# A feed-forward part whose second product is issued inside the next batch's first phase

## The reference, cut to what matters

```python
def act_quant(x):      # per token, to int8 steps
    scale = 127.0 / jnp.clip(jnp.max(jnp.abs(x), axis=-1, keepdims=True), 1e-05)
    return jnp.clip(jnp.round(x * scale), -128, 127) / scale
def weight_quant(w):   # to -1, 0, 1
    scale = 1.0 / jnp.clip(jnp.mean(jnp.abs(w)), 1e-05)
    return jnp.clip(jnp.round(w * scale), -1, 1) / scale
def _L0_ffn_ref(x, w1, conv_w, conv_b, w2):      # x is already layer-normed
    h = bit_linear(x, w1)                        # (4, 1024, 512) -> (4, 1024, 2048)
    h = depthwise_conv1d(h.transpose(0, 2, 1), conv_w, conv_b)   # 3 taps over tokens
    h = jax.nn.silu(h.transpose(0, 2, 1))
    return bit_linear(h, w2)                     # -> (4, 1024, 512)
x = x + jnp.tanh(g_ffn[0]) * _L0_ffn_ref(_layernorm(x), ...)
```

## Time and profile before

| | us |
|---|---|
| median of the three runs | 1868.02 |
| the profiled execution, its time | 1868.89 |
| its span in the profile | 1867.1 |
| TensorE busy | 1669.6 (89%) |
| VectorE busy | 1204.4 (65%) |
| ScalarE busy | 827.8 (44%) |
| GpSimd busy | 719.0 (39%) |
| mean granted TensorE clock | 0.965 of full |

### The profile page before, as it was taken

One profiled execution on the slowest core, in us unless ns is written; L12 is line 12 of the kernel. 1 busy time (PEld: TensorE's weight loads), 2 busy tenths in 40 slices (PEclk: granted clock), 3 DMA queues, 4 the chain that ended last, 5 costly groups with the idle time before them and its releaser, 6 DMA issues. The chain is left out here.

```text
span 1867.1 us, 23800 instructions
## 1 busy us (share of the span) xinstructions
PE 1669.6 (89%) x8754; PEld 1026.6 (55%) x8754; DVE 1204.4 (65%) x2205; ACT 827.8 (44%) x866; POOL 719.0 (39%) x314
## 2 busy tenths in 40 slices
PE   6888899999999999999999999999986876877758
PEld 5666678888886544454445444544453433444434
DVE  6777645443345667657865786667359478399793
ACT  2111222222220344424562456345647767677666
POOL 1131000000000488856875687567825043151340
PEclk9999999999999999999999999999999897998989
DMA  6656456544434411202231213221331020200201
GB/s 238 238 186 213 168 193 223 176 160 152 157 130 158 148 58 67 98 20 103 98 106 48 102 59 113 69 103 36 128 136 53 23 90 23 89 2 1 91 0 46
DMA packets 107811, 200.81 MB, mean 108 GB/s; under 512 B 7616, under 2 KB 33216, under 8 KB 107712
## 3 DMA queue, kind: packets, MB, share of 16 engines
q1 hardware_dynamic: 107712, 199.49, 30.4%
HBM read 124.75 MB, written 74.71 MB: 107 GB/s over the span
## 5 line engine op out<-in xcount | busy, mean ns | idle before, releaser
L726 POOL TENSOR_TENSOR acc<-acc,pr 128x1024 f32<-128x1024 f32 x188 | 448.3, 2385 | 134.4 <-ACT pr L756 117.8
L756 ACT ACTIVATE pr<-ps,mcol 128x1024 f32<-128x1024 f32 x256 | 284.4, 1115 | 366.5 <-PE ps L1452 363.9
L1014 DVE CUSTOM_DVE_ANT_0 junk<-ps,mbias 128x512 bf16<-128x512 f32 x512 | 333.1, 688 | 129.3 <-PE ps L1427 125.2
L1464 PE MATMUL ps<-pr,vv 128*64 128x512 f32 x1024 | 274.7, 618 | 0.0
L731 POOL TENSOR_TENSOR h_first<-h_first,last_tap 128x1024 f32<-128x1024 f32 x44 | 104.8, 2386 | 274.0 <-ACT last_tap L897 274.0
L707 POOL MEMSET nmt<- 128x128 f32 x1 | 0.2, 204 | 364.2 <-DVE chl L1227 364.2
L1427 PE MATMUL ps<-kh,qh 64*128 64x512 f32 x512 | 123.0, 452 | 13.1 <-DVE nmv L1014 12.0
L1533 PE MATMUL ps<-xiT,w1q 128*128 128x512 bf16 x512 | 123.8, 389 | 5.0 <-ACT xiT L746 5.0
L726 POOL TENSOR_TENSOR acc<-pr 128x1024 f32<-128x1024 f32 x32 | 76.8, 2401 | 122.0 <-ACT pr L756 122.0
L1427 PEld LDWEIGHTS ps<-kh,qh 64*128 64x128 f32 x512 | 51.0, 185 | 130.9 <-issue 99.3
L1690 PE MATMUL ps<-w2q,hq 128*128 128x512 bf16 x512 | 121.2, 390 | 1.5 <-ACT hq L925 0.8
(11 more groups left out here) (173 smaller groups left out, 3218.8 us busy)
## 6 DMA issues: line engine op xcount, KB each, us to landing
craw<-in_ctxT SPq DMA_DIRECT2D x8, 2048.0 KB, 9.6
xa<-in_x SPq DMA_DIRECT2D x8, 1024.0 KB, 6.2
wraw<-in_w1T SPq DMA_DIRECT2D x16, 512.0 KB, 7.6
wraw<-in_w2T SPq DMA_DIRECT2D x16, 512.0 KB, 8.1
q_split<-kqh SPq DMA_DIRECT2D x32, 256.0 KB, 2.0
q_split<-kql SPq DMA_DIRECT2D x32, 256.0 KB, 2.3
base<-lna SPq DMA_DIRECT2D x8, 1024.0 KB, 9.1
k_split<-kqh SPq DMA_DIRECT2D x32, 256.0 KB, 2.1
```

The costliest lines, as they stand in the source:

```text
L726: nc.gpsimd.tensor_tensor(acc[:, blk % 2, :], first, pr[:, (8 * blk + j) % NP, :], ALU.add).then_inc(pool_acc, 1)
L756: act.activation(pr[:, u % NP, :], ps[:, 2 * (u % 2):2 * (u % 2) + 2, :].rearrange("p a t -> p (a t)"), ACT.Exp, bias=mcol[:, (u // 64) * ...
L1014: dve.tensor_tensor_reduce(out=(junk1 if n < LEAD and n % 2 else junk)[:, e, :], in0=ps[:, first_bank(n) + e, :], in1=mbias[:, b % 2, kk * ...
L1464: last = pe.matmul(ps[64 * e:64 * e + 64, 6 + blk % 2, :], vv[g % 2][:, j, 64 * e:64 * e + 64], pr[:, u % NP, e * CH:(e + 1) * CH], start= ...
```

## The change

A batch's second product is no longer a phase of its own. In the first phase of the next batch, block j issues half of a token tile of the previous batch's second product: the half q = j, eight transposes (`turn_h(b - 1, j)`), a copy (`turned`) and eight matmuls (`second(b - 1, j - 1)`, one block later). Only the last batch's second product stands alone, in half tiles too. The rounded hidden values are kept for a whole batch, as int8 in `h8`, which VectorE writes straight from `hT` in eight instructions between two first phases; GpSimd converts them to bfloat16 (`to_bf16`), a token tile at a time, in two buffers `hb`.

The convolution works on PSUM: `dve_scaled` writes back into the pair of banks, the taps read from there (`pair(j)`), shifted by slices and without padding, and `gp` is gone. VectorE's tap now comes before GpSimd's add, and `pe_first` of block j + 2 waits for VectorE's tap of block j. The turns of `h` use banks 4 and 5 only; bank 6 takes in turn the halves of `turn_h`, the halves of the next batch's row and the turns of its input; bank 7 takes the second product.

`row` and `xiT` become two buffers each. The next batch's row and turns stand in blocks 8 to 13 of the first phase. The eight layer-norm steps of batch 3 stand in the first phase of batch 0, after blocks 1, 2 and 4 to 9 (`STEP_AT`), and its integers go through DRAM as those of the other batches do. `x2` is loaded and the output stored a token tile at a time. In the diff only added and kept lines are shown, since the removed ones stand above.

```diff
+        row = [sb("row0", [P, S], F32), sb("row1", [P, S], F32)]
+        xiT = [sb("xiT0", [P, KD, S], BF16), sb("xiT1", [P, KD, S], BF16)]
+        h = [sb("h_first", [P, S], F32), sb("h_second", [P, S], F32)]
+        assert used["at"] <= CHL + SLOT
         used["at"] = CHL + SLOT
         x2 = sb("x2t", [P, NT, D], F32)
         used["at"] = XN
+        h.append(sb("h_third", [P, S], F32))
+        last_tap = [sb("last_tap0", [P, S], F32), sb("last_tap1", [P, S], F32)]
+        LAST_NORM = used["at"]
+        h8 = sb("h8", [P, NT, HID], INT8)
...
+        STEP_AT = (1, 2, 4, 5, 6, 7, 8, 9)
+        STD_AT = 4
...
+        def pair(j):
+            return ps[:, 2 * (j % 2):2 * (j % 2) + 2, :].rearrange("p a t -> p (a t)")
...
+            def load_x2(b, i):
+                r = (b * NT + i) * P
+                sp.dma_start(x2[:, i, :], x2_d[r:r + P, :]).then_inc(sp_x2_in[i], 16)
+
+            for i in range(NT):
+                load_x2(0, i)
             load_xn(B - 1)
+            for b in range(B + 1):
+                if b + 1 < B:
+                    sp.wait_ge(pe_xt, (b + 1) * (NT // 2))
                     load_xi(b + 1)
+                if b == 0:
+                    sp.wait_ge(dve_ln, LN_DVE_N)
+                    sp.dma_start(xi_d[(B - 1) * S:B * S, :].rearrange("(j p) d -> p j d", p=P), xi3[:]).then_inc(sp_xi_out, 16)
+                    continue
+                for i in range(NT):
+                    r = ((b - 1) * NT + i) * P
+                    sp.wait_ge(dve_d, D_DVE[f"o{b - 1}_{i}"])
+                    sp.dma_start(out[r:r + P, :], x2[:, i, :]).then_inc(sp_out, 16)
+                    if b < B:
+                        sp.wait_ge(sp_out, 16 * ((b - 1) * NT + i + 1))
+                        load_x2(b, i)
+            sp.wait_ge(sp_out, 16 * B * NT)
...
+            def to_bf16(b, i):
+                pool.wait_ge(dve_d, D_DVE[f"q{b}_{i}"])
+                if i >= 2:
+                    pool.wait_ge(pe_ht, b * KH + 2 * i - 2)
+                elif b:
+                    pool.wait_ge(pe_ht, b * KH - 2 + 2 * i)
+                nc.gpsimd.tensor_copy(hb[:, i % 2, :], h8[:, i, :]).then_inc(pool_bf, 1)
+
+            for b in range(B):
                 for j in range(KH):
+                    pool.wait_ge(act_d, D_ACT[f"u{b}_{j}"])
+                    pool.wait_ge(dve_d, D_DVE[f"c{b}_{j}"])
+                    nc.gpsimd.tensor_tensor(h[(b * KH + j) % 3][:, 0:S - 1], h[(b * KH + j) % 3][:, 0:S - 1], last_tap[j % 2][:, 0:S - 1], ALU.add).then_inc(pool_tap, 1)
+                    if b and j % 2 == 0 and 2 <= j < KH - 2:
+                        to_bf16(b - 1, j // 2 + 1)
+                to_bf16(b, 0)
+                to_bf16(b, 1)
+            for i in range(2, NT):
+                to_bf16(B - 1, i)
...
+            def taps(b, j):
+                act.wait_ge(dve_d, D_DVE[f"g{b}_{j}"])
+                if b * KH + j >= 3:
+                    act.wait_ge(pe_ct, b * KH + j - 2)
+                act.activation(h[(b * KH + j) % 3][:], pair(j), ACT.Identity, bias=convb[:, j:j + 1],
+                               scale=convw[:, j, 1:2]).then_inc(act_d, 1)
+                if b * KH + j >= 2:
+                    act.wait_ge(pool_tap, b * KH + j - 1)
+                act.activation(last_tap[j % 2][:, 0:S - 1], pair(j)[:, 1:S], ACT.Copy, scale=convw[:, j, 2:3]).then_inc(act_d, 1)
+
+            def turned(b, q):
+                i, t = q // 2, q % 2
+                act.wait_ge(pe_ht, b * KH + q + 1)
+                if b * NT + i >= 2:
+                    act.wait_ge(pe_o, b * NT + i - 1)
+                act.activation(hq[:, i % 2, 8 * t:8 * t + 8].rearrange("p j t -> p (j t)"), ps[:, 6, :].bitcast(BF16),
+                               ACT.Copy).then_inc(act_d, 1)
+
+            taps(0, 0)
+            taps(0, 1)
+            for b in range(B):
                 for j in range(KH):
                     if j + 2 < KH:
+                        taps(b, j + 2)
                     act.wait_ge(pe_ct, b * KH + j + 1)
+                    if b and j == 0:
+                        act.wait_ge(dve_d, D_DVE[f"q{b - 1}_{NT - 1}"])
+                    act.activation(hT[:, :, j * P:(j + 1) * P], ps[:, 4:6, :].rearrange("p a (i t) -> p (a i) t", t=P),
                                    ACT.Silu).then_inc(act_d, 1)
+                    if b:
+                        turned(b - 1, j)
+                    if b == 0 and j == STD_AT:
+                        act_ln_std(act, B - 1)
+                    if b + 1 < B and j in (8, 9):
+                        act_ln_row(act, b + 1, j - 8)
+                    if b + 1 < B and 10 <= j < 10 + NT // 2:
+                        act_ln_turned(act, b + 1, j - 10)
+                if b + 1 < B:
+                    taps(b + 1, 0)
+                    taps(b + 1, 1)
+            for q in range(KH):
+                turned(B - 1, q)
...
+            steps = ln_steps(dve, B - 1)
+            for b in range(B):
                 for j in range(KH):
+                    done(f"g{b}_{j}")
+                    dve.wait_ge(act_d, D_ACT[f"u{b}_{j}"])
+                    dve.scalar_tensor_tensor(out=h[(b * KH + j) % 3][:, 1:S], in0=pair(j)[:, 0:S - 1], scalar=convw[:, j, 0:1], in1=h[(b * KH + j) % 3][:, 1:S],
+                                             op0=ALU.mult, op1=ALU.add).then_inc(dve_d, 1)
+                    if j >= 2:
+                        biggest(b, j - 2)
+                    if b and j >= 3 and j % 2:
+                        finish2(b - 1, (j - 3) // 2)
                     if j + 2 < KH:
                         dve_scaled(dve, b, j + 2)
+                    if b == 0 and j in STEP_AT:
+                        steps[STEP_AT.index(j)]()
+                    if b + 1 < B and j == 6:
+                        dve.wait_ge(pe_row, 2 * b + 1)
+                        dve_diagonal(dve, b + 1)
+                if b + 1 < B:
+                    dve_scaled(dve, b + 1, 0)
+                biggest(b, KH - 2)
+                biggest(b, KH - 1)
+                if b:
+                    finish2(b - 1, NT - 1)
+                    done(f"o{b - 1}_{NT - 1}")
+                done(f"hmax{b}_{KH - 1}")
                 dve.tensor_reduce(hm[:], hmax[:].rearrange("p j i -> p i j"), AX.X, ALU.max).then_inc(dve_d, 1)
+                done(f"hm{b}")
                 dve.tensor_scalar(hm[:], hm[:], 1e-5, None, ALU.max).then_inc(dve_d, 1)
+                done(f"hmc{b}")
                 dve.reciprocal(hsc[:], hm[:]).then_inc(dve_d, 1)
+                done(f"hrec{b}")
                 dve.tensor_scalar(hsc[:], hsc[:], 127.0, None, ALU.mult).then_inc(dve_d, 1)
                 dve.tensor_scalar(hdq[:], hm[:], deq2, None, ALU.mult).then_inc(dve_d, 1)
+                done(f"hdq{b}")
+                if b:
+                    dve.wait_ge(pool_bf, b * NT)
+                else:
+                    dve.wait_ge(sp_xi_out, 16 * B)
                 for i in range(NT):
+                    dve.tensor_scalar(h8[:, i, :], hT[:, i, :], hsc[:, i:i + 1], None, ALU.mult).then_inc(dve_d, 1)
+                    if i == 1 and b + 1 < B:
+                        dve_scaled(dve, b + 1, 1)
+            for i in range(NT):
+                finish2(B - 1, i)
...
+            if b == 0:
+                for t in range(2):
+                    last = pe.matmul(ps[:, 2 + t, :], ones[:], diag[:, 4 * t:4 * t + 4, :], start=True, stop=True)
+                last.then_inc(pe_row, 1)
+            else:
+                pe.matmul(ps[:, 6, :], ones[:], diag[:, 4 * half:4 * half + 4, :], start=True, stop=True).then_inc(pe_row, 1)
...
+                pe.wait_ge(dve_d, D_DVE[f"c{b}_{j - 2}"])
+            elif b:
+                pe.wait_ge(dve_d, D_DVE[f"c{b - 1}_{KH - 2 + j}"])
+            if b and j == 0:
+                pe.wait_ge(act_ln, LN_ACT[f"xT{b}_{NT // 2 - 1}"])
             for t in range(2):
                 for k in range(KD):
+                    last = pe.matmul(ps[:, 2 * (j % 2) + t, :], w1q[:, k, j * P:(j + 1) * P], xiT[b % 2][:, k, t * 512:(t + 1) * 512],
...
+            def turn_h(b, q):
+                i, t = q // 2, q % 2
+                if t == 0:
+                    pe.wait_ge(pool_bf, b * NT + i + 1)
+                for j in range(8 * t, 8 * t + 8):
+                    last = pe.transpose(ps[:, 6, :].bitcast(BF16)[:, (j % 8) * P:(j % 8 + 1) * P], hb[:, i % 2, j * P:(j + 1) * P], identb[:])
+                last.then_inc(pe_ht, 1)
+
+            def second(b, q):
+                i, t = q // 2, q % 2
+                pe.wait_ge(act_d, D_ACT[f"hq{b}_{q}"])
+                if t == 0 and b * NT + i:
+                    pe.wait_ge(dve_d, D_DVE[f"o{b}_{i - 1}" if i else f"o{b - 1}_{NT - 1}"])
+                for j in range(8 * t, 8 * t + 8):
+                    last = pe.matmul(ps[:, 7, :], hq[:, i % 2, j, :], w2q[:, j, :], start=j == 0, stop=j == KH - 1)
+                if t:
+                    last.then_inc(pe_o, 1)
+
+            def turn_free(b, j, last_use):
```

(80 more changed lines are left out.)

285 lines of the change are left out of this document (65 added, 220 removed).

## The result

| | kernel before | kernel after |
|---|---|---|
| median, us | 1867.98 (1863.62 to 1870.0, 4 runs) | 1929.57 (1926.86 to 1933.58, 4 runs) |
| profiled execution, us | 1868.89 | 1933.58 |
| span of the profile, us | 1867.1 | 1931.8 |

The changed kernel takes 1.0335 times as long (95% interval 1.0306 to 1.0363), 62 us more. The forecast was 1916.5 in a range of 1878 to 1945: the sign and the mechanism came out, the size is 13 us short of the median.

A forecast was written before the change was run, and what follows sets the result against it. Bound: a chain of waits through all engines, 5.20 us a block. Batch 0 to 1508.5, two batches of 117.7, batch 3's 88.6, tail 63.1: 1895.6; casts 9, clock 11: span 1915.6, forecast 1916.5, range 1878 to 1945.

The forecast's parts named there:

- one chain of waits through all engines: Blocks of batches 1 to 3: waits running through the engines and back take 10.40 us per two blocks, 5.20 each.
- the clock term: TensorE falling to 1.2 GHz after waits: 11 us in all, 1.5 of it after xn; between nothing and 25.
- Blocks without a norm step: Batch 0's first phase: VectorE's taps and TensorE's first product wait on each other, 4.38 us a block against 4.05.
- the stall: Batch 0, before the first layer-norm statistics: VectorE stands waiting for the DMA of xn, 14.1 us.
- The blocks with row halves: Blocks in batches 1 and 2 issuing half of the next batch's row, waiting for ScalarE's copy: 8.15 us each.
- those with a turn: Blocks in batches 1 and 2 turning the next batch's input, waiting for ScalarE's copy: 7.77 us each.
- Roundings and casts: Batch ends: eight roundings and VectorE's next tap 12.0 us; GpSimd's casts beside them 3 more, three times, 9 in all.
- the rival of roundings at one column a cycle: Batch ends: int8 roundings of 2048 columns take 2.35 us, giving 1942; chance 0.10.
- Tail: Last batch's second product standing alone: 3.46 us a half block with one turn bank, against 2.17; sum 63.1.
- PE is never late behind ScalarE: Rival: blocks at TensorE's own 4.84 us, tail at 2.17 a half block, giving 1854, faster; chance 0.10.
- Slow casts: Rival: GpSimd's casts as slow as its two-input add, 4.8 us each, giving 1937; chance 0.06.
- xn in time: Rival for batch 0: xn lands in time or its wait costs half, 1902 to 1909; no separate chance given.

The follow-up runs named there:

- the two edits together: Kernel after, last batch's second product only: turn of h issued before the product, and output accumulators alternating between banks 7 and 0; 1911.52 us, ratio 1.0236.
- the kernel with all remedies: Kernel after with turns before products, row halves and turns right behind F, layer-norm steps later, casts behind the last rounding, two output banks in the tail; 1848.97 us.

## Why the prediction was right, and where it fell short

The forecast of 1915.6 for the span stands against 1931.8. The mechanism held: one chain of waits through all engines sets each block. The step that was mis-sized is a term of the sum, the clock in batch 0. By stretches:

| term, casts and clock put in | forecast | measured |
|---|---|---|
| C(0) of batch 0 ends | 1387.9 | 1388.65 |
| batch 0 to its first rounding | 110.1 | 122.4 |
| roundings to C(0), three times | 45.1 | 42.3 |
| batches 1 and 2, to the first rounding | 216.2 | 223.5 |
| batch 3, likewise | 91.1 | 89.35 |
| tail | 65.1 | 65.6 |

**Batch 0, the step that was mis-sized: the clock term.** Its parts came out where they had been put. Blocks without a norm step 4.41 (4.38), and the stall, forecast at 14.1:

```profile
1409.96 2.47 DVE L984 BATCH_NORM_STATS2 st<-xn 128x6 f32<-128x512 f32 x4 [13.68 <-DMA xn<-x]
1412.35 1.27 DVE L1365 SCALAR_TENSOR_TENSOR h_third<-ps,convw,h_third 128x1023 f32<-128x1023 f32 x1
...
1413.68 3.59 PE L1562 MATMUL ps<-xiT,w1q 128*128 128x512 bf16 x8 [16.01 <-DVE h_third L1365]
```

(xn was issued at 1398.26 and is what ends VectorE's idle time; C(2) and F(4) stand behind.) But the last row shows F at 3.59 where 1.89 was put, the lower level of the clock, 1.2 GHz. The forecast gave 1.5 us to this clock after the stall and named the gaps of the norm steps only for the upper end. The granted clock was 0.68 and 0.74 over 78 us: F waits for C, C for a norm step, TensorE stands about half of each block, and F, on the chain, takes 1.1 to 1.7 more in seven of the blocks. From C(0) to C(14) that made 109.1 against 98.4. In the run with matmuls without use this part took 99.9, near the forecast without the clock term: the gain came with the raised clock, while VectorE's steps stayed as they were. The other 3 us of batch 0 lie at its end, from C(14)'s end to the first rounding 13.3 against 10.2: F(1,0) waited for the last turn's copy, behind t, u and silu on ScalarE, a wait that the forecast had counted for batches 1 and 2 and left out for batch 0.

```profile
1499.59 1.03 ACT L797 ACTIVATE xiT<-ps 128x1024 bf16<-128x1024 bf16 x1
...
1500.76 1.01 PE L1562 MATMUL ps<-xiT,w1q 128*128 128x512 bf16 x2 [3.35 <-ACT xiT L797]
```

**Blocks of batches 1 to 3.** The chain was worked out at 5.20 and measured at 5.17, and the doubled copy lengthened it. The blocks with row halves were worked out at 8.15 and came at 8.25. Of those with a turn (7.77) one came at 7.75 and two at 9.42 and 9.06 in batch 1, the clock again; in these F stands behind the wait for K, and it took 3.21:

```profile
1601.68 0.62 PE L1434 MATMUL ps<-identb,xi 128*128 128x128 bf16 x8 [2.35 <-ACT hq L952]
1602.14 3.21 PE L1562 MATMUL ps<-xiT,w1q 128*128 128x512 bf16 x8
```

The three take 26.2 in batch 1 and 25.8 in batch 2 where 23.3 was put, most of the 3.6 by which each of these batches went over; the rest lies in their first blocks and ahead of the rounding. Moving these items showed that this part was the dearest of the change: forecast at 17 over plain blocks in each of two batches, 37 in all once they no longer bar F.

**Roundings and casts.** 14.1 at each batch end, where 12.0 and 3 for the casts had been put. From the timeline of the kernel after:

```profile
1511.04 2.48 DVE L1400 TENSOR_SCALAR h<-hT,hsc 128x2048 int8<-128x2048 f32 x2
1512.39 5.71 POOL L768 CAST hb<-h 128x2048 bf16<-128x2048 int8 x2 [9.73 <-DVE h L1400]
...
1514.57 9.39 DVE L1400 TENSOR_SCALAR h<-hT,hsc 128x2048 int8<-128x2048 f32 x6
...
1525.30 2.29 PE L1562 MATMUL ps<-xiT,w1q 128*128 128x512 bf16 x5 [17.81 <-DVE h_second L1365]
```

The roundings beside a cast took up to 2.91, the others 1.28, and with the casts behind them none was stretched: 2.1 per batch end. The two casts and the two stretched roundings one by one, from the same timeline:

```profile
1512.39 2.88 POOL L768 CAST hb<-h 128x2048 bf16<-128x2048 int8 x1 [9.73 <-DVE h L1400]
...
1514.57 1.78 DVE L1400 TENSOR_SCALAR h<-hT,hsc 128x2048 int8<-128x2048 f32 x1
...
1515.22 2.89 POOL L768 CAST hb<-h 128x2048 bf16<-128x2048 int8 x1
...
1516.27 2.91 DVE L1400 TENSOR_SCALAR h<-hT,hsc 128x2048 int8<-128x2048 f32 x1
```

They take turns, at all three batch ends alike. Each of these roundings ends 1.07 or 1.08 after the cast that it met (1516.35 after 1515.27, 1519.18 after 1518.11), just as the old C ended 1.08 after the add, and each cast ends 1.75 or 1.76 after the rounding that it met (the second rounding ends at 1513.52). So a rounding does wait as C did. The two casts cost 2.1 and not 4.2 because the first ran mostly beside G (from 1513.44 on), which works on PSUM and kept its 1.23: it cost the roundings 0.5, the second cost them 1.6. The rule of the Trainium skill that the forecast had weighed (GPSIMD Engine Reference, section Specifications: GpSimd's SBUF interfaces are contended by VectorE's two-port modes) is borne out by these rows. The rival of roundings at one column a cycle fell with 1.28, as the Trainium skill (Vector Engine (DVE) Microarchitecture Reference, section Performance modes) would have it: there the two-port mode asks for both operands in SBUF and not for a width.

**Tail.** Between two K's lie 3.46 (3.46 forecast), from the timeline of the kernel after:

```profile
1894.34 1.02 ACT L952 ACTIVATE hq<-ps 128x1024 bf16<-128x1024 bf16 x1 [2.44 <-PE ps L1678]
...
1897.81 1.02 ACT L952 ACTIVATE hq<-ps 128x1024 bf16<-128x1024 bf16 x1 [2.44 <-PE ps L1678]
```

The price of the order and of the single bank had been put at 19 against the old kernel's 2.17; the two edits together gave 17.2 of the tail back, to 2.17 per half block. The start had been put at 5.5, though its own terms (1.3, 2.1, H and K) give some 5.2; the first product began 6.5 after the first rounding.

**The rivals.** "PE is never late behind ScalarE", priced at 1854, did not happen: the blocks of batch 3 came at 5.17 and not at 4.84, and at 5.72 with the copy doubled. That the kernel with all remedies comes to 1849 does not bear it out either. Some 21 us of its gain lie in the norm's steps and the casts, which this rival left as they were, and its plain blocks still take 5.00 and not 4.84. Slow casts and xn in time did not occur.

**A reading that was wrong.** The forecast calls VectorE nearly idle in a second phase; the earlier trace rows show it busy for 27.4 of 60.0 us. No term of the sum rests on that.

**What stays open.** Why two turn blocks of a batch run at the lower clock and others don't, and why this moved when only the order of T and S changed, no run settles. What the tap on PSUM is worth alone was not tried; the traces show only its price (1.27 against a median of 2.01) and that it binds F to C.

## What to carry to other kernels

Before laying one phase over another, write down each engine's queue and follow one period around through all engines; the period of that loop, not the busiest engine's sum, is the time per block, and an item placed ahead of the loop's instruction costs its whole wait each time. Place extra work behind the instruction that starts the loop (here worth 37 us), put the turn ahead of the product (10 us in the tail), and give the accumulator a second bank where nothing else needs it (8 us more). A wait put on a chain can cost twice when it also empties TensorE: after the stall the next F ran at the lower clock, 3.59 for 1.89.
